# First turn of a fused cross-attention and expert kernel: x ahead of the biases, new order of setup work on VectorE and GpSimd

## What is computed

```python
h = layernorm(x)
q = rms_norm(h @ q_w.T + q_b) * norm_q_w          # 16 heads of 16
k = rms_norm(ctx @ k_img_w.T + k_img_b) * norm_k_img_w
v = ctx @ v_img_w.T + v_img_b
a = softmax(q k^T / 4) @ v                        # per sequence and head
x = x + a @ o_w.T + o_b
# experts: 8, the two best of each row
h = layernorm(x)
probs = softmax(h @ gate_w.T); top 2, renormalised
x = x + sum over 2 experts of weight * ((silu(g) * u) @ w2[e].T),  g, u = h @ w1[e].T
```

## Time and profile before

| | us |
|---|---|
| three runs | 474.77, 475.24, 473.72 |
| their median | 474.77 |
| the profiled execution, its own time | 472.38 |
| its span, first to last instruction | 470.6 |
| PE busy | 432.7 (92%) |
| DVE busy | 382.6 (81%) |
| ACT busy | 290.2 (62%) |
| POOL busy | 283.5 (60%) |

### The profile page before, as it was taken

How to read it: one execution, slowest core, us unless ns; L and a number is a source line. 1 busy time by engine, 2 the same in 40 slices (tenths; PEclk the granted TensorE clock), 3 DMA queues, 4 the chain that set the end, 5 groups by cost and what they waited for, 6 DMA issues and landing times.

```text
span 470.6 us, 15198 instructions
## 1 busy us (share of the span) xinstructions
PE 432.7 (92%) x4428; PEld 381.3 (81%) x4428; DVE 382.6 (81%) x1352; ACT 290.2 (62%) x802; POOL 283.5 (60%) x472
## 2 busy tenths in 40 slices
PE   6699999999999999989999998799999999998980
PEld 2468888898989889778888886489999999888870
DVE  7555888989898989889989886689777777898993
ACT  5246676777777767667667754555665656565550
POOL 6934437777686777667768665674444444454451
PEclk9999999999999999999999999999999999999996
DMA  7225544243333434223343333555443435889965
GB/s 214 82 74 150 150 133 132 80 119 92 110 105 94 121 92 119 87 80 107 87 108 108 92 86 101 140 186 153 125 135 120 126 114 172 248 250 308 323 195 171
DMA packets 55514, 64.62 MB, mean 137 GB/s; under 512 B 9599, under 2 KB 49034, under 8 KB 55434
## 3 DMA queue, kind: packets, MB, share of 16 engines
q1 hardware_dynamic: 44602, 42.59, 32.6%
q0 software_dynamic: 6480, 16.85, 10.3%
q10 hardware_dynamic: 4352, 4.20, 2.6%
HBM read 32.73 MB, written 23.14 MB: 119 GB/s over the span
## 4 chain that ended last, share of the span: by engine, by line
PE 80%; DVE 6%; issue 6%; POOL 5%; DMA 1%; ACT 1%; POOLq 0%; DVEq 0%; SPq 0%; ACTq 0%
PE bank L1352 14%; PE bank L1354 13%; PE bank L1353 12%; PE bank L1593 5%; PE bank L1413 4%; PE bank L1360 3%; PE bank L1401 3%; PE bank L1466 3%; PE bank L1462 3%; PE bank L1464 3%; PE bank L1463 3%; PE bank L1378 3%; PE bank L1385 2%; PE bank L1626 2%; PE bank L1625 2%
## 5 line engine op out<-in xcount | busy, mean ns | idle before, releaser
L608 POOL DMA_INDIRECT expert_out<-probs,late x71 | 72.9, 1026 | 75.3 <-ACT probs L797 72.4
L541 POOL DMA_INDIRECT sorted_rows<-row,place_i x64 | 68.4, 1068 | 34.7 <-POOL row L533 24.5
L1352 PE MATMUL bank<-we_h,xt_h 128*128 x142 | 51.9, 365 | 2.0 <-DVE xt_l L1266 2.0
L701 ACT ACTIVATE probs<-bank 128x1024 f32<-128x1024 f32 x32 | 32.9, 1027 | 23.3 <-PE bank L1466 23.3
L785 ACT ACTIVATE xn<-bank 128x176 f32<-128x176 f32 x71 | 22.6, 318 | 38.8 <-PE bank L1354 38.8
L1354 PE MATMUL bank<-we_h,xt_l 128*128 x142 | 45.7, 322 | 0.0
L1353 PE MATMUL bank<-we_l,xt_h 128*128 x142 | 45.7, 322 | 0.0
L1276 DVE SCALAR_TENSOR_TENSOR probs<-xn,late,bank 128x128 f32<-128x128 f32 x71 | 24.4, 344 | 19.9 <-ACT xn L785 19.3
L929 DVE TENSOR_REDUCE bank<-bank 128x16 f32<-128x1024 f32 x32 | 39.1, 1222 | 0.0
L797 ACT COPY probs<-bank 128x256 f32<-128x256 f32 x71 | 26.5, 373 | 16.6 <-PE bank L1626 16.2
L1466 PE MATMUL bank<-neg_max_t,head_of 128*128 128x128 bf16 x256 | 35.2, 219 | 0.0
(11 more groups left out here) (233 smaller groups left out, 1586.2 us busy)
## 6 DMA issues: line engine op xcount, KB each, us to landing
late<-sorted_rows SPq DMA_DIRECT2D x71, 129.0 KB, 2.3
we_f<-w_exp SPq DMA_DIRECT2D x32, 152.0 KB, 2.3
v_bd<-v_sb SPq DMA_DIRECT2D x128, 34.0 KB, 2.3
ctx_in<-ctx_t SPq DMA_DIRECT2D x32, 128.0 KB, 2.4
qp<-q_hl SPq DMA_DIRECT2D x128, 32.0 KB
x<-x SPq DMA_DIRECT2D x3, 1024.0 KB, 5.6
row<-expert_out SPq DMA_DIRECT2D x6, 512.0 KB, 5.3
qp<-expert_out SPq DMA_DIRECT2D x6, 512.0 KB, 4.7
```

Of the source, the lines that this page charges most:

```text
L541: pool.indirect_dma_start(sorted_rows, bass.IndirectOffsetOnAxis(ap=place_i[:, t.slot // 2, k, t.par:t.par + 1], axis=0), row[:, k, t.slot ...
L608: pool.indirect_dma_start(expert_out, bass.IndirectOffsetOnAxis(ap=hs(r)[:, D:D + 1].bitcast(U32), axis=0), y_sb[:, r % YRING, :], None, b ...
L1352: pe.matmul(dst, a_h, b_h, start=start, stop=False)
```

## The change

All of it concerns setup and turn 0.

- ACT: `ln1_norm(0)` and `split_hi(1)` come straight behind `ctx_hi(0)`. The two bias instructions, now `bias_parts`, come in turn 0 behind `xt_hi(0)`.
- DVE: `split_lo(0)` ends the first part. In turn 0, behind `xt_lo(0)`: `split_lo(1)`, `split_biases`, `join_norms`. The statistics of tiles 2 and 3 move from before `fold_gate` to behind the three scaling operations of tile 0.
- PE: the bias matmul leaves `project` for `add_bias`. In turn 0 `project_q` waits for 11 steps and `project_kv` for 12, and only the bias matmuls wait for 14, the one of q (`end_project_q`) standing behind `project_kv`. In all other turns the matmuls come in the order of before.
- POOL: `ctx_lo(0)` comes before `ln_roots(1)`. The selects over `head_of` and `ident_b` go to the end of turn 0 (`rest_of_setup`). `qk_rms(0)` comes first in turn 0, ahead of `ln_roots(2)` and `ctx_lo(1)`.
- SP: the waits for the whole setup are gone from before turn 0; the store of padding rows, with the wait for POOL's setup, stands at the head of turn 3.

```diff
-    SETUP_DVE_QK = 13
+    SETUP_DVE_QK = 11
+    SETUP_DVE_VO = 12
+    SETUP_DVE_BIAS = 14
...
-        sp.wait_ge(dve_setup, SETUP_DVE)
-        sp.wait_ge(pool_setup, SETUP_POOL)
-        sp.dma_start(sorted_rows[NE * REG:ROWS, :], pad_rows[:, :]).then_inc(pads_sent, 16)
+        def send_last_pads():
+            sp.wait_ge(pool_setup, SETUP_POOL)
+            sp.dma_start(sorted_rows[NE * REG:ROWS, :], pad_rows[:, :]).then_inc(pads_sent, 16)
 
         def turn(j, s):
+            if j == 0 and s == 3:
+                send_last_pads()
...
         def turn(j, s):
+            if j == s == 0:
+                qk_rms(Tile(0, 0))
             if Tile(j, s + 2).live or Tile(j, s - 4).live:
                 ln_roots(Tile(j, s + 2), Tile(j, s - 4))
...
-            if Tile(j, s).live:
+            if Tile(j, s).live and not j == s == 0:
                 qk_rms(Tile(j, s))
...
             if Tile(j, s).live:
                 weights_lo(Tile(j, s))
+            if j == s == 0:
+                rest_of_setup()
...
         ln_roots(Tile(0, 0), Tile(0, -6))
+        ctx_lo(Tile(0, 0))
         ln_roots(Tile(0, 1), Tile(0, -5))
-        ctx_lo(Tile(0, 0))
-        for base in (0, -NH):
...
-        setup(pool.tensor_copy(ident_b[:, :], ident[:, :]))
...
                 xt_hi(tile(0))
+            if j == s == 0:
+                bias_parts()
...
         split_hi(0)
         ctx_hi(t)
-        act.wait_ge(bias_loaded, 16)
...
-        act.activation(bias_f, bias_f, ACT.Copy, scale=zero_one[:, 1:2]).then_inc(bias_parts_ready, 1)
         ln1_norm(t)
         split_hi(1)
...
-            if isinstance(j, int) and j == s == 0:
-                ln1_stats(tile(-2), x_second)
-                ln1_mean(tile(-2))
-            if ahead:
+            if ahead and not j == s == 0:
...
                 q_scale(tile(0))
+            if j == s == 0:
+                for t in (tile(-2), tile(-3)):
+                    ln1_stats(t, x_second if t.n == 2 else None)
+                    ln1_mean(t)
...
         split_lo(0)
-        split_biases()
...
         def rest_of_setup():
+            split_lo(1)
+            assert done[0] == SETUP_DVE_VO, done[0]
+            split_biases()
+            assert done[0] == SETUP_DVE_BIAS, done[0]
             join_norms()
-            split_lo(1)
...
+
+        def add_bias(dst, m, cols):
             return pe.matmul(dst, ones_row[:, :], bias_hl[:, m, 0:cols], start=False, stop=True)
...
             if t.first:
-                pe.wait_ge(dve_setup, SETUP_DVE)
...
+                pe.wait_ge(dve_setup, SETUP_DVE_VO)
+            dst = kv_bank[:, 0:2 * D].rearrange("p (m d) -> p m d", m=2)
+            project(dst, ct_h[:, t.par], ct_l[:, t.par], slice(KM, VM + 1), D)
+            if t.first:
+                pe.wait_ge(dve_setup, SETUP_DVE_BIAS)
+            add_bias(dst, slice(KM, VM + 1), D).then_inc(S["k_projected"], 1)
...
+            project(qp_bank[:, 0:DG], xt_h[:, t.par], xt_l[:, t.par], QM, DG)
+            if not t.first:
+                end_project_q()
+
+        def end_project_q():
+            add_bias(qp_bank[:, 0:DG], QM, DG).then_inc(S["projected"], 1)
...
                 project_kv(t)
+                end_project_q()
                 gate_fold()
```

More of the change, by code:

```diff
@@ L559, in turn, with rest_of_setup @@
                 weights_lo(Tile(j, s))
+            if j == s == 0:
+                rest_of_setup()
+        def rest_of_setup():
+            for base in (0, -NH):
+                after()
+                v = head_of[0:2 * NH, :, :].rearrange("r g (q m) -> r g q m", q=2)
+                setup(pool.affine_select(out=v, in_=v, compare_op=ALU.not_equal, fill=1.0, base=base,
+                                         pattern=[[-2, NPAIR], [-1, 2], [0, L]], channel_multiplier=1))
+            setup(pool.tensor_copy(ident_b[:, :], ident[:, :]))
+            assert done[0] == SETUP_POOL, done[0]
         setup(pool.memset(ident[:, :], 0.0))
@@ L599, in _ @@
         setup(pool.iota(pad_rows[:, D:D + 1].bitcast(I32), [[0, 1]], base=2 * T, channel_multiplier=1))
-        assert done[0] == SETUP_POOL, done[0]
         pool.memset(qp[:, :, :, :, :, :, :].rearrange("p u g n c b l -> p (u g n c b l)").bitcast(F32), 0.0
@@ L754, in _, with bias_parts @@
         t.at = 0
+        def bias_parts():
+            act.wait_ge(bias_loaded, 16)
+            act.wait_ge(bias_cleared, 1)
+            act.copy(bias_hl[0:2, :, 0:D], bias_f).then_inc(bias_parts_ready, 1)
+            act.wait_ge(pool_setup, SETUP_POOL_FIRST)
+            act.activation(bias_f, bias_f, ACT.Copy, scale=zero_one[:, 1:2]).then_inc(bias_parts_ready, 1)
         split_hi(0)
         ctx_hi(t)
-        act.wait_ge(bias_loaded, 16)
-        act.wait_ge(bias_cleared, 1)
-        act.copy(bias_hl[0:2, :, 0:D], bias_f).then_inc(bias_parts_ready, 1)
-        act.wait_ge(pool_setup, SETUP_POOL_FIRST)
-        act.activation(bias_f, bias_f, ACT.Copy, scale=zero_one[:, 1:2]).then_inc(bias_parts_ready, 1)
         ln1_norm(t)
@@ L1422, in project_kv @@
             if t.first:
-                pe.wait_ge(dve_setup, SETUP_DVE)
-            project(kv_bank[:, 0:2 * D].rearrange("p (m d) -> p m d", m=2), ct_h[:, t.par], ct_l[:, t.par],
-                    slice(KM, VM + 1), D).then_inc(S["k_projected"], 1)
+                pe.wait_ge(dve_setup, SETUP_DVE_VO)
[4 more added lines that the diff above has]
+            add_bias(dst, slice(KM, VM + 1), D).then_inc(S["k_projected"], 1)
         def project_q(t):
@@ L1433, in project_q @@
             pe.wait_ge(S["xt_l_ready"], t.n + 1)
-            project(qp_bank[:, 0:DG], xt_h[:, t.par], xt_l[:, t.par], QM, DG).then_inc(S["projected"], 1)
+            project(qp_bank[:, 0:DG], xt_h[:, t.par], xt_l[:, t.par], QM, DG)
[3 more added lines that the diff above has]
+            add_bias(qp_bank[:, 0:DG], QM, DG).then_inc(S["projected"], 1)
         def tr_max(t):
@@ L1474, in project_out @@
                 pe.wait_ge(S["neg_max_t_ready"], t.max_read)
-            project(mo_bank[:, 0:DG], at_h[:, t.par], at_l[:, t.par], OM, DG).then_inc(S["o_projected"], 1)
+            project(mo_bank[:, 0:DG], at_h[:, t.par], at_l[:, t.par], OM, DG)
+            add_bias(mo_bank[:, 0:DG], OM, DG).then_inc(S["o_projected"], 1)
         def gate_mean():
```

## The result

| | before | after |
|---|---|---|
| median of all runs side by side (19 each) | 473.92 us | 471.36 us |
| lowest to highest | 470.73 to 477.05 | 469.12 to 474.17 |
| the profiled execution | 472.38 | 469.28 |
| its span | 470.6 | 467.5 |

The ratio of after to before is 0.9944, 95% interval 0.9917 to 0.9970: 0.56% faster, about 2.6 us. I had forecast 473.7 from a median of 474.77, that is 1.1 us, with a range from 471.4. The change goes the way of the forecast, but its size was more than twice the forecast. The base of the forecast, the median of three runs, was 0.85 above that of all 19 (473.92), so the times themselves stand further apart than the gains.

A forecast was written before the change was run, and what follows sets the result against it. PE was taken as the bound (80% of the chain), with POOL setting the start. `tr_k(1)` 2.8 us earlier less 1.7 for a low clock gave 1.1 us off the median 474.77: 473.7 us, range 471.4 to 475.4.

The forecast's parts named there:

- wait for the biases on PE: Turn 0, PE's new wait before the bias matmuls: hidden, by 0.2 us at worst.
- my bound of 1.75: DVE's bias sum in turn 0: starts near 12.3, takes at most 1.75 us, there by 14.0.
- the debt falls due in the second turn: POOL's second turn: late statistics and moved setup delay its queue; `qk_rms(1)` at 25.95, `tr_k(1)` at 27.5, 2.8 us earlier.
- a setup of 2.5 and one of 4.6: `head_of` and `ident_b` on POOL in the second turn: 2.5 us of work taken, 4.6 as upper bound.
- I take a low clock again, at the 1.71 priced above: PE after its pause from 25.1 to 27.5: low clock costs 1.71 us, bounds nothing and 2.0.
- what the change takes off the second is what the rest of the kernel, bound by PE, begins earlier: Second milestone, start of `tr_k(1)`: its 2.8 us lead passes to the rest of the kernel.
- The clock stays full: Rival: no low clock after the pause before `tr_k(1)`, the whole 2.8 us arrives, 472.0 us; chance 0.24.
- Setup held: Rival: second-turn `head_of` and `ident_b` cost the full 4.6 us; 1.0 slower, 475.8 us; chance 0.12.
- Lost later: Rival: a later turn is bound by another fixed-time wait, such as a load; nothing arrives, 474.8 us; chance 0.12.

The follow-up runs named there:

- after_again: The changed kernel once more, unchanged, in another single execution; 469.27 us.
- front_part_only: The changed kernel with POOL's order and the place of DVE's statistics put back as before the change; 474.76 us, ratio 1.0041 to the kernel before.
- after_beside: The changed kernel once more, unchanged, for comparison on the same chip as later variants; 471.75 us, ratio 0.9950 to the kernel before.
- pool_part_only: The kernel before with only POOL's new order, the late statistics and SP's change; 474.53 us, ratio 1.0009.
- before_again: The kernel before once more, unchanged, in another single execution; 472.71 us.
- setup_late: The changed kernel with `head_of` and `ident_b` one turn later and PE's wait for them at first use; 471.31 us, ratio 0.9930 to the kernel before.
- both_moves: The changed kernel with tile 2's statistics ahead of `fold_gate` and `head_of`, `ident_b` one turn later; 468.17 us, ratio 0.9859 to the kernel before.
- both_beside: both_moves once more, unchanged, for comparison on the same chip; 471.17 us, ratio 0.9928 to the kernel before.
- stats_early: The changed kernel with tile 2's statistics put back ahead of `fold_gate`; 471.07 us, ratio 0.9934 to the kernel before.
- three_moves: both_moves with SP issuing the 1 MB load of x one turn earlier; 468.12 us, ratio 0.9893 to the kernel before.
- pause_bare: The changed kernel with none of the 8 warm-up matmuls before `tr_k(1)`; 474.34 us, ratio 1.0005 to the kernel before.

## Why the prediction was right and where it was wrong

Against the steps of the sum:

| step | forecast | after | |
|---|---|---|---|
| query projection | 10.91 | 10.49 | 11.43 and 10.76 in the other two executions; the load of the weights lands at other times |
| key/value projection | 12.73 | 11.98 | |
| wait for the biases on PE | none, by 0.2 | none | |
| gate fold | 14.57 | 13.91 | |
| `k_scale(0)` | 16.7 | 15.98 | |
| `tr_k(0)` | 17.3 | 16.50 | 17.45 and 16.79 in the other two executions |
| roots of tile 2 begin | 18.4 | 17.74 | |
| `head_of` and `ident_b` | 21.4, 2.5 long | 20.44, 2.70 long | |
| `qk_rms(1)` | 25.95 | 25.28 | |
| `tr_k(1)` | 27.5 | 26.84 | 27.80 and 27.14 in the other two |
| pause before it | 25.1 to 27.5, 2.4 | 2.60 | 2.61 and 2.61 in the other two |
| low clock after it | yes, 1.7 | none | 1.5 in one of three |
| the rest of the kernel begins earlier by | the lead at `tr_k(1)` | 0.6 more | |

**Right.** The order of the steps and what each waits for. ACT's timeline of the changed kernel has

```profile
6.52 1.04 ACT L763 CAST wp_h<-probs 128x1024 fp32r<-128x1024 f32 x1 [4.43 <-DMA probs<-w_proj]
...
9.51 0.37 ACT L633 CAST xt_h<-bank 128x256 fp32r<-128x256 f32 x1
```

where the earlier trace rows had `xt_hi` at 11.59. The bias sum on DVE took less than my bound of 1.75:

```profile
11.98 1.27 DVE L910 SCALAR_TENSOR_TENSOR bias_hl<-bias_hl,zero_one,row 2x1024 fp32r<-2x1024 f32 x1 [0.45 <-ACT row L773]
```

It ended at 13.25, ahead of the bias matmuls at 13.56, 0.3 us of margin where I had 0.2. That the profile shown came 0.4 to 1.0 earlier than the forecast at every step up to `tr_k(1)` is in part luck with the opening loads: after_again has `tr_k(1)` at 27.80, 0.3 later than forecast. That the debt falls due in the second turn, on POOL, was right to a few tenths. The choice between a setup of 2.5 and one of 4.6 was the right one: 2.70 from 20.44 to 23.14. The rule of the Trainium skill ("SBUF — State Buffer", section "Who interferes with whom") spoke for the lower value, since no DVE operation with two SBUF inputs stands beside `head_of` there. (Its other half, that an operation with one SBUF input or none blocks nothing, the page limits to operations outside VectorE's 2-port modes, which my prediction left out.) The rows agree: `head_of` took 2.46 instead of the 3.45 of the earlier trace rows. In front_part_only, where the selects stand in their old place beside DVE's splits, the two took 3.25 and `ident_b` 1.59 instead of 0.28.

**Wrong, first step:** "I take a low clock again, at the 1.71 priced above". This term took the forecast gain from 2.8 down to 1.1 us; measured were 2.6. Over a pause of 2.60 or 2.61 us the clock fell in after_beside and pool_part_only, and held in after and after_again: two of four. When it fell, it cost 1.50 and 1.62 (9.06 and 9.18 against 7.56), so the size was about right and the certainty wrong. The 1.71 had been read from one execution, where it cost 1.07 by the milestones; before_again shows the kernel before without that fall. I had this case as a rival with a chance of 0.24; an even chance would have been nearer to what the four executions show. The rule of thumb of the Trainium skill ("TensorE: Matmul & The Clock Gate", section "HAM oscillation — how this bites in real kernels"), that such a pause would be too short to bring the clock down, is not borne out as a promise either: two of four fell.

**Wrong, second step:** "what the change takes off the second is what the rest of the kernel, bound by PE, begins earlier". It isn't, in either kernel. In the kernel before, `score_max(1)` waited for the spreading behind the 1 MB load, 0.57 with the fall of the clock in front of it and 1.58 without: the fall was almost free, because the wait behind the load took back what PE had won without it (39.35 and 39.14, where `tr_k(2)` was 1.23 apart). So I subtracted a fall from the new kernel, where it costs, and compared with a kernel in which its own fall cost next to nothing. In the changed kernel the pause delays the spreading out of the load's way, and the lead grows from 3.50 to 4.14. I had the DMA issues of SP in the profile and followed them only where the change touched them; this load stands next to the spreading in SP's queue, and I did not ask what the one does to the other.

**How the parts add up** between the two profiled executions: 3.50 at `tr_k(1)`, 0.01 more at `tr_k(2)`, 0.63 more at `score_max(1)`, 4.31 at the transposes of x for tile 31 (271.93 against 267.62), 3.96 where ACT starts `xt_h` of the first expert slot (298.82 against 294.86), 3.10 at the end. In between the lead was not constant: the next load of x cost the changed kernel a wait of 1.10 at `score_max(3)` (52.34) where the kernel before waited 0.41, and the one after it cost the kernel before 0.93 at `score_max(5)` and the changed kernel nothing. The low clock at 299 to 303, which the kernel before had not, took nothing off the lead (3.93 at the sixth slot); most of what was lost went after 400 us, for a reason that I haven't found. With the fall, after_beside, the lead is 3.20, 1.71, 2.35 at the same three places, 2.82 at the transposes of x for tile 7 and 1.84 at those for tile 8. In between it met a load again: the third one, issued at 63.84, the spreading at 64.53, and in PE's timeline

```profile
71.10 0.64 PE L1421 MATMUL bank<-late,qp 128*64 128x128 f16 x16 [1.91 <-issue]
```

At tile 31 1.40 is left. The median gain, 2.6, lies between such executions.

**The rivals.** "The clock stays full" was half of the truth: its gain of 2.8 is next to the 2.6 measured. That the two agree so well is in part luck, since the lead of the three profiled executions of the changed kernel at tile 31 is 4.31, 3.40 and 1.40. Its time of 472.0 lies above the 471.36 measured only because it starts from 474.77; from 473.92 it would be 471.1. "Setup held" did not happen: 2.70, under the 3.6 from which it decides. "Lost later" did not happen in the changed kernel, but its mechanism, a load a turn later, is exactly what took back the gains of setup_late and both_moves. I had looked for it in the chain after 31 us. There the wait of 0.57 shows only as a step of ACT (38.60, 0.59 us, line 634) between `tr_k(2)` and `score_max(1)`, not as one of a DMA.

**The range** ended at 471.4, built as full clock with half a microsecond of spread below 474.77 less 2.8; from 473.92 the same range would have ended at 470.6. Both kernels spread more than that by themselves, 469.12 to 474.17 in 19 runs of after, and the median of before alone moved between 473.03 and 474.76 from one set of runs to the next.

## What to carry to other kernels

Follow a lead for two or three turns, past the first milestone, and ask at each load which transfers queue right behind it: a pause can cost little while it keeps a large load and the small urgent DMAs apart, and here its removal was shown to pay only together with moving the load (0.9893 against 0.9950; with the load in place, 0.9928, it is open). Price a fall of the clock over a pause of 2 to 3 us as a chance, and look at a second execution of the unchanged kernel before putting a number from one low stretch into the sum. If an engine is to be relieved at the start, move both what comes to it late and what it does in the meantime: here each half alone gained nothing.

## What the runs showed of the hardware that I had not expected

The granted clock falls or holds over the same 2.6 us pause from one execution to the next (after, after_beside), and one low stretch moved from 22 to 26 to 12 to 16 between two executions of the kernel before, there behind a pause of only 1.41 us (before PE's start at 10.68). Every low stretch between 10 and 60 us in these traces came within 2 us behind a pause of PE of 1.41 to 3.67 us, or within the one of 4.34; and pauses of 1.49 to 1.79 and two of 2.6 had none. The low stretch of the 4.34 us pause lasted 6.5 us, the others some 3.5.

The small DMAs that spread the query are late when the 1 MB load stands shortly ahead of them in SP's issues. From the issue of the first of the four to `score_max(1)`:

| | load to spreading | spreading to `score_max(1)` | wait of PE |
|---|---|---|---|
| setup_late | 1.06 | 6.32 | 2.13 |
| both_beside | 1.14 | 5.68 | 1.49 |
| front_part_only | 1.27 | 5.51 | 1.32 |
| both_moves | 1.28 | 5.52 | 1.33 |
| before_again | 1.72 | 5.76 | 1.58 |
| before | 1.97 | 4.76 | 0.57 |
| stats_early | 3.22 | 4.70 | 0.51 |
| after | 4.23 | 4.12 | none |
| three_moves | load a turn earlier | 4.12 | none |

For this load nothing is left of it at a distance of 4 us; under 2 us it cost between half a microsecond and two. The distance alone doesn't settle it. Two more loads of 1 MB follow, in turns 3 and 5, 0.7 to 3.6 us ahead of the spreading of tiles 3 and 5. At distances of 1.86 to 1.90 us the wait behind the first of them was none in after_again, after_beside and three_moves, 1.10 in after and 1.78 in pause_bare. Their order was not changed in any experiment; three_moves still waits 1.01 us at 65.61.
